# Joint attention of a four-layer gated network, rewritten for products of two rounded parts, two query halves beside each other and steps of two key tiles

## The reference, cut to what matters

```python
H = 16; head_dim = 16
q = x @ Wq + bq
k = concatenate([x @ Wks + bks, context @ Wkc + bkc], axis=1)    # 1024 + 154 keys
v = concatenate([x @ Wvs + bvs, context @ Wvc + bvc], axis=1)
attn = softmax(einsum('bhqd,bhkd->bhqk', q, k) / sqrt(16))
out = einsum('bhqk,bhkd->bqhd', attn, v)
x = x + tanh(gate) * (out @ Wo + bo)
```

## Time and profile before

| | |
|---|---|
| Median of 3 runs (lowest to highest) | 3018.72 us (3017.26 to 3019.69) |
| Profiled execution, time | 3019.72 us |
| Profiled execution, span | 3017.8 us |
| Busy PE / DVE / ACT / POOL | 80% / 66% / 42% / 31% |
| Mean granted TensorE clock | 0.878 of 2.4 GHz |

### The profile page before, as it was taken

One profiled execution on the slowest core, in us unless ns is written; L12 is line 12 of the kernel. 1 busy time (PEld: TensorE's weight loads), 2 busy tenths in 40 slices (PEclk: granted clock), 3 DMA queues, 4 the chain that ended last, 5 costly groups with the idle time before them and its releaser, 6 DMA issues. The chain is left out here.

```text
span 3017.8 us, 43014 instructions
## 1 busy us (share of the span) xinstructions
PE 2415.8 (80%) x15716; PEld 1650.5 (55%) x15716; DVE 1999.3 (66%) x4265; ACT 1255.4 (42%) x2974; POOL 937.4 (31%) x867
## 2 busy tenths in 40 slices
PE   6799999987997899759999776888888987950254
PEld 3233333336886566548888444777666776840122
DVE  4588888824766555457776346775657675579898
ACT  4266666642443544323333112646325564320121
POOL 2000000001554433225554002554335453413343
PEclk9799999996998999869999677899898998975566
DMA  1111111101001000110000001000100000010000
GB/s 71 23 27 27 30 27 27 30 19 47 1 1 58 1 1 1 41 68 1 1 1 4 22 1 47 1 1 12 68 1 1 2 1 32 1 42 0 0 1 28
DMA packets 15681, 57.90 MB, mean 19 GB/s; under 512 B 7408, under 2 KB 7408, under 8 KB 13552
## 3 DMA queue, kind: packets, MB, share of 16 engines
q1 hardware_dynamic: 15472, 55.15, 5.5%
HBM read 39.37 MB, written 2.10 MB: 14 GB/s over the span
## 5 line engine op out<-in xcount | busy, mean ns | idle before, releaser
L2298 ACT ACTIVATE probs<-psum 128x512 f32<-128x512 f32 (+1 forms) x640 | 346.7, 593 | 195.9 <-PE psum L2242 195.0
L2313 DVE TENSOR_REDUCE max_parts<-psum 128x1 f32<-128x512 f32 x512 | 328.6, 684 | 63.4 <-PE psum L2215 59.6
L152 PE MATMUL psum<-x_upper,weights_upper 128*128 128x512 f32 (+2 forms) x624 | 252.8, 405 | 26.6 <-POOL weights_rest L164 17.6
L152 PE MATMUL psum<-x_rest,weights_upper 128*128 128x512 f32 (+2 forms) x624 | 249.8, 400 | 0.0
L152 PE MATMUL psum<-x_upper,weights_rest 128*128 128x512 f32 (+2 forms) x624 | 247.1, 396 | 0.0
L152 PE MATMUL psum<-weights_upper,hidden_upper 128*128 128x256 f32 (+2 forms) x768 | 242.4, 316 | 1.8 <-DVE x_tok L311 1.7
L164 POOL TENSOR_TENSOR weights_rest<-L1f,weights_upper 128x256 fp32r<-128x256 f32 x216 | 181.4, 866 | 183.6 <-ACT weights_upper L269 183.6
L152 PE MATMUL psum<-weights_upper,hidden_rest 128*128 128x256 f32 (+2 forms) x768 | 217.2, 283 | 0.0
L152 PE MATMUL psum<-weights_rest,hidden_upper 128*128 128x256 f32 (+2 forms) x768 | 217.1, 283 | 0.0
L2253 PE MATMUL psum<-probs,v_tok 128*17 128x256 f32 (+1 forms) x2560 | 201.1, 385 | 0.4 <-ACT probs L2298 0.4
L2242 PE MATMUL psum<-q_stack,k_stack 98*128 98x512 bf16 (+1 forms) x640 | 198.3, 387 | 0.5
(11 more groups left out here) (432 smaller groups left out, 6065.4 us busy)
## 6 DMA issues: line engine op xcount, KB each, us to landing
L1f<-in_L1f SPq DMA_DIRECT2D x1, 7936.0 KB, 21.6
k_stack<-k_parts SPq DMA_DIRECT2D x192, 36.8 KB, 2.0
q_stack<-q_parts SPq DMA_DIRECT2D x192, 32.0 KB, 2.0
L0f<-in_L0f SPq DMA_DIRECT2D x1, 4760.0 KB, 14.4
L2f<-in_L2f SPq DMA_DIRECT2D x2, 2268.0 KB, 8.5
L1x<-in_L1x SPq DMA_DIRECT2D x1, 4226.0 KB, 13.2
L2a<-in_L2a SPq DMA_DIRECT2D x2, 2048.0 KB, 11.4
L3f<-in_L3f SPq DMA_DIRECT2D x1, 3072.0 KB, 10.2
```

The source lines that it names most:

```text
L152: ins = pe.matmul(out, lhsT(a).bitcast(F32R), rhs(b).bitcast(F32R), start=start and n == 0, stop=stop and n == len(PASSES) - 1, skip_group ...
L2298: act.activation(pb[0:m, s % NPB, hf * 512:(hf + 1) * 512], net.ps[0:m, STB + hf, :], ACT.Exp, scale=HD ** -0.5).then_inc(exp_done, 1)
L2313: v.tensor_reduce(mx3[:, u % 2, q, k:k + 1], net.ps[:, XB + (2 * n + k) % 3, :], AX.X, ALU.max).then_inc(x_taken, 1)
```

## The change

- Parts. q and k are split into two parts in fp32r. The stack has three combinations of 16 rows (48), and the two rows of maxima make 50.
- Halves. Queries 0 to 511 stand on partitions 0 to 49 of the stack, queries 512 to 1023 on 64 to 113, with the keys copied to both. So each product is two of 512 columns, one for each half, into banks of their own. Stacking a unit still takes 12 transfers: 6 of queries (16 rows x 2 KB) and 6 of keys (16 rows x 4.7 KB, before 2.4 KB). The maxima take four transfers, one per part and half.
- Steps. The five steps of a unit hold two key tiles each: a pair of maxima, two tiles of scores, a pair of maxima, turns, then the value products of the step before's two tiles. Maxima, turned maxima and turned results share a ring of three banks. Four pairs of unit u+2 stand in steps 3 and 4 of unit u, in front of the turn and the split of unit u+1's maxima.
- Exponentials take 1024 columns from two banks. ScalarE also copies the result of a unit out and, once turned, into `o_raw`; dividing by the sum is left to the end of a batch (GpSimd for the first, VectorE for the second).
- Projections and output are three products of rounded parts; biases are added while the results are taken, the output's bias by GpSimd under the heads. The projections go batch by batch, x is transposed there, and the stacks of units 0 to 2 are sent meanwhile.
- The output weights and the context by token become packs of their own (`L0o`, `L3c`); `L3c` is loaded before the last layer.

```diff
--- before.py
+++ after.py
@@ -2049,323 +2058,517 @@
     KT = [P] * (S // P) + CT
     NK = len(KT)
     HC = P // HD
-    Q_PARTS, K_PARTS = [0, 0, 0, 1, 1, 2], [0, 1, 2, 0, 1, 0]
+    Q_PARTS, K_PARTS = [0, 0, 1], [0, 1, 0]
     ROWS = HD * len(Q_PARTS)
+    HALF = 64
...
-        qp = net.sb(attn, "q_parts", [P, 3, C, B, S], BF16)
-        kp = net.sb(attn, "k_parts", [P, 3, C, B, KEYS], BF16)
+        vt = net.sb(attn, "v_tok", [P, B, NK, H, HD + 1])
+        qs = net.sb(attn, "q_stack", [P, NST, S // 2])
+        ks = net.sb(attn, "k_stack", [P, NST, KEYS])
+        qp = two(attn, "q_parts", [P, C, B, S])
+        kp = two(attn, "k_parts", [P, C, B, KEYS])
...
+        def stack(sp, u):
+            b, h = head(u)
+            c, r0 = h // HC, (h % HC) * HD
+            s = u % NST
+            for r, (i, j) in enumerate(zip(Q_PARTS, K_PARTS)):
+                for e in range(2):
+                    lo = HALF * e + r * HD
+                    sp.dma_start(qs[lo:lo + HD, s, :], qp[i][r0:r0 + HD, c, b, e * 512:(e + 1) * 512])\
+                        .then_inc(stacked[s], 16)
+                    sp.dma_start(ks[lo:lo + HD, s, :], kp[j][r0:r0 + HD, c, b, :]).then_inc(stacked[s], 16)
...
+            w = Weights(net, ctx, "L0x")
+            w_out.load()
...
+            layer_norm(net, x, None, keep=xn)
...
+            @block.sync
+            def _(sp):
+                sp.wait_ge(ones_in, 3)
+                sp.wait_ge(taken, 5)
+                for u in range(NST):
+                    stack(sp, u)
...
-                        ins = pe.matmul(net.ps[:, n % 4, 0:m], wt[:, k, c * P:(c + 1) * P], src(k),
-                                        start=k == 0, stop=k == C - 1)
+                        ins = three(pe, net.ps[:, IB + n % 4, 0:m], [p[:, k, c * P:(c + 1) * P] for p in wp[name]],
+                                    [p[:, k, :] for p in src], k == 0, k == C - 1)
                     ins.then_inc(made, 1)
...
+                for b in range(B):
+                    turn_x(b)
+                    for n in range(PER):
+                        project(b * PER + n)
+                    for k in range(NK):
+                        values(b, k)
...
+                    for n in range(b * PER, (b + 1) * PER):
+                        _, bias, c, _, out, m = items[n]
+                        v.wait_ge(part_upper, n + 1)
+                        v.scalar_tensor_tensor(out[1].bitcast(F32R), net.ps[:, IB + n % 4, 0:m], w(bias)[:, c:c + 1],
+                                               out[0], ALU.add, ALU.subtract).then_inc(taken, 1)
+                    v.wait_ge(ones_in, 1)
+                    for k in range(NK):
+                        m = KT[k]
+                        v.wait_ge(v_made, b * NK + k + 1)
+                        heads = lambda ap: ap.rearrange("p (h d) -> p h d", d=HD)
+                        v.tensor_tensor(vt[0:m, b, k, :, 0:HD], heads(net.ps[0:m, VB + k % 4, 0:D]),
+                                        heads(w("bvs" if k < S // P else "bvc")[0:m]), ALU.add).then_inc(v_taken, 1)
...
+            NPB, STEPS, AHEAD = 4, NK // 2, 4
+            ST, RING, NR, PVB = 0, 4, 3, 7
...
+            pairs = [("self", j, k) for j in range(4) for k in range(2)] + [("ctx", i, 0) for i in range(2)]
+            NPAIR = len(pairs)
+            ring = [("max", 0, i, e) for i in range(NPAIR) for e in range(2)] + [("top", 0)]
+            ring += [("max", 1, i, e) for i in range(AHEAD) for e in range(2)]
+            at_step = {}
+            for u in range(NU):
+                for k in range(STEPS):
+                    n = u * NPAIR + NPAIR + AHEAD + 2 * k
+                    here = [divmod(m, NPAIR) for m in (n, n + 1) if m < NU * NPAIR]
+                    at_step[u, k] = here
+                    for v_, i in here:
+                        ring += [("max", v_, i, e) for e in range(2)]
+                    if k == 2 and u > 0:
+                        ring.append(("out", u - 1))
+                    if k == 3 and u + 1 < NU:
+                        ring.append(("top", u + 1))
+            ring.append(("out", NU - 1))
...
                 for u in range(NU):
...
+                    n = place["top", u]
+                    sp.wait_ge(reduced, n + 1 - outs_before[n])
...
+                        for e in range(2):
+                            row = HALF * e + ROWS + r
+                            sp.dma_start(qs[row:row + 1, s, :], part[4 * e:4 * e + 4, u % 2, :]).then_inc(rows_in[s], 16)
+                    if u >= 1 and u + 2 < NU:
+                        sp.wait_ge(st_done, 2 * NK * u)
+                        stack(sp, u + 2)
...
+                def enter(item):
+                    n = place[item] - NR
+                    if n >= 0:
+                        if ring[n][0] == "out":
+                            pe.wait_ge(out_taken, outs_before[n] + 1)
+                        else:
+                            pe.wait_ge(reduced, n + 1 - outs_before[n])
+                def max_pair(u, i):
                     s = u % NST
+                    kind, a, k = pairs[i]
+                    if i == 0:
                         pe.wait_ge(stacked[s], 12 * 16 * (u // NST + 1))
...
+                    for e in range(2):
+                        enter(("max", u, i, e))
+                    if kind == "self":
+                        for e in range(2):
+                            r = slice(HALF * e, HALF * e + ROWS)
+                            pe.matmul(bank(("max", u, i, e)), qs[r, s, a * P:(a + 1) * P].bitcast(F32R),
+                                      ks[r, s, k * 512:(k + 1) * 512].bitcast(F32R), start=True, stop=True)\
+                                .then_inc(made, 1)
...
                 def turn_max(u):
+                    enter(("top", u))
+                    pe.wait_ge(max_done, u + 1)
+                    pe.transpose(bank(("top", u))[0:QT, 0:P], mx[:, u % 2, :], net.ident[:]).then_inc(made, 1)
...
                 def scores(u, k):
...
+                        pe.wait_ge(rows_in[s], 64 * (u // NST + 1))
+                    if n >= 2:
+                        pe.wait_ge(exp_done, n - 1)
+                    for e in range(2):
+                        r = slice(HALF * e, HALF * e + ROWS + 2)
+                        pe.matmul(net.ps[0:m, ST + 2 * (k % 2) + e, :], ks[r, s, k * P:k * P + m].bitcast(F32R),
+                                  qs[r, s, :].bitcast(F32R), start=True, stop=True).then_inc(st_done, 1)
...
+                    pe.wait_ge(exp_done, n + 1)
+                    if k == 0 and u > 0:
+                        pe.wait_ge(o_copied, u)
...
+                for u in range(NU):
+                    for k in range(STEPS):
+                        here = at_step[u, k]
+                        for v_, i in here[:1]:
+                            max_pair(v_, i)
+                        scores(u, 2 * k)
+                        scores(u, 2 * k + 1)
+                        for v_, i in here[1:]:
+                            max_pair(v_, i)
+                        if k == 2 and u > 0:
+                            turn_out(u - 1)
+                        if k == 3 and u + 1 < NU:
+                            turn_max(u + 1)
+                        n = u * STEPS + k - 1
+                        if n >= 0:
+                            for m in range(2):
+                                weighted(n // STEPS, 2 * (n % STEPS) + m)
...
+                        n, m = u * NK + k, KT[k]
+                        if n >= NPB:
+                            act.wait_ge(pv_done, n - NPB + 1)
+                        act.wait_ge(st_done, 2 * (n + 1))
+                        act.activation(pb[0:m, n % NPB, :], net.ps[0:m, ST + 2 * (k % 2):ST + 2 * (k % 2) + 2, :]
+                                       .rearrange("p a n -> p (a n)"), ACT.Exp, scale=HD ** -0.5).then_inc(exp_done, 1)
+                        if k == 1 and u > 0:
+                            copy_out(u - 1)
+                        if k == 5 and u > 0:
+                            take_out(u - 1)
...
+                    for e in range(2):
+                        v.wait_ge(made, place["max", u, i, e] + 1)
...
+                def split_max(u):
+                    if u >= 2:
+                        v.wait_ge(rows_in[(u - 2) % NST], 64 * ((u - 2) // NST + 1))
+                    v.wait_ge(made, place["top", u] + 1)
+                    src = bank(("top", u))[0:QT, 0:P]
+                    v.tensor_scalar(hi[:, u % 2, :].bitcast(F32R), src, -1.0, None, ALU.mult).then_inc(hi_done, 1)
+                    v.wait_ge(hi_done, u + 1)
+                    v.scalar_tensor_tensor(lo[:, u % 2, :].bitcast(F32R), src, -1.0, hi[:, u % 2, :], ALU.mult,
+                                           ALU.subtract).then_inc(reduced, 1)
...
+                for u in range(NU):
+                    for k in range(STEPS):
+                        for v_, i in at_step[u, k]:
+                            reduce_pair(v_, i)
```

(56 more changed lines are left out.)

536 lines of the change are left out of this document (270 added, 266 removed).

## The result

The changed kernel takes 2999.36 us (median of 14 runs, 2987.94 to 3014.72), the kernel before 3018.41 in runs on the same chips: ratio 0.9941, 95% interval 0.9925 to 0.9956. So it is faster by 0.6%, where 2.3% was forecast, and its time lies above the range. Its runs spread over 27 us; the fastest had a mean granted clock of 0.865, the slowest of 0.851. The profiled execution took 2995.63 us.

A forecast was written before the change was run, and what follows sets the result against it. TensorE's column stream bounded the old kernel; SyncE's queue would bound the new heads. Start -33.3, heads -27.0, output -12.5, later stages +1.3 gave -71.5 from 3019.72: 2948 us, range 2895 to 2992.

The forecast's parts named there:

- the chain through SyncE: Heads: sending maxima 2.9, stacking issues 6.9, landing 2.1, then 3.44 to the next send make 15.5 us a unit.
- The projections: Start of the kernel: shorter TensorE work, ending at 73.2 us, first maximum at 75.2, stacks of units 0 to 2 hidden underneath.
- The output: Output projection after the heads: 20.3 us, where it took 32.8 before, a gain of 12.5.
- units 1 to 29 at 15.5: Heads: each of these units takes 15.5 us between sends of maxima, 449.5 in all; before, 16.11 a unit.
- rival A: The main forecast, SyncE's queue closing the loop in the heads: 2948 us, own range 2933 to 2963; 50%.
- T(0): Moment SyncE starts to send unit 0's maxima: forecast 88.3 us, was 121.58, with 13.1 from first maximum as before.
- T(0) to T(1): Start of the heads, from sending unit 0's maxima to sending unit 1's: 13.8 us, as stacks are already there.
- rival E: Heads: TensorE's clock falls to its lower level for good, a unit takes some 20 us, total 3078; 10%.
- Without SyncE's chain 13.8: Heads: if SyncE's queue did not close the loop, a unit would take 10.35 + 3.44 = 13.8 us.
- Rival B: Heads: the queue does not close the loop, the unit falls to 13.8 us, total 2899; 14%.
- Rival C: Heads: half-height products don't overlap for 50 rows of 512 columns, unit about 16.3 us, total 2971; 12%.
- Rival D: Heads: stacks land later because key rows are larger, up to 1.5 us a unit, total 2991; 14%.

The follow-up runs named there:

- turn_single: Changed kernel with the next unit's maxima turned before the wait for stacks, and each half of a maxima pair waiting only for its own bank: 2916.56 us, ratio 0.966.
- half_stacks: Changed kernel, from unit 3 on sending only the six stacking transfers of the first row half: 2951.59 us, ratio 0.9778.
- start_busy: Changed kernel with unread filler products at the start of the heads, five before the first maximum and four after each of unit 0's pairs: 2998.59 us, ratio 0.9939.
- turn_first: Changed kernel with step 3 turning and splitting the next unit's maxima before the first pair of maxima of unit u+2: 2943.69 us, ratio 0.9758.
- turn_fill: turn_first with two unread products between the bank waits of each self maxima pair and five at the start: 3024.92 us, ratio 1.0027.
- split_pool: Changed kernel with the six stacking transfers of the second row half sent from GpSimd's queue instead of SyncE's: 3022.69 us, ratio 1.0012.
- turn_spread: turn_single with value products of one key tile between the halves of each step's second maxima pair: 3026.93 us once, 3222.5 three times.

## Why the prediction was wrong

The direction of the whole and the chain through SyncE were right; the time was 51 us too low, and in the heads the direction was wrong. That the kernel is faster all the same comes from the start and the output, not from the heads. Step by step:

- **The projections** were right: first maximum at 75.06, forecast 75.2, the stacks ready under them. **The output** took 22.8, forecast 20.3; two low stretches of 3.4 us lie in it. Before it took 33.7 (640.71 to 674.4), where the sum has 32.8. **Later stages** took 2.4, forecast 1.3.
- **The step that failed: units 1 to 29 at 15.5.** The chain itself (rival A) is confirmed: 15.62 to 15.64 in undisturbed units, 0.63 a transfer up and down, and gone when the pair is moved behind the turn. But the average was 16.63: 29 x 1.13 = 33 of the 51 us (against the profiled runs, 47 us; T(0), T(0) to T(1), the output and the later stages make up the rest). The chain's own 0.12 a unit is 3.5 us of them. Two terms were put at nothing. The first is the clock, rival E, in a milder form than forecast: stretches of 3.4 to 20.5 us at 0.50 and not the whole of the heads. They cost about 14 us: 11.2 in seven units, in which TensorE came late to the pair that needs the stacks, and 2.4 between that pair and the next send. The idling in the waits lets the clock fall: filled, it was 1.00; lengthened, it was lower. I had set little on E by the cross attention, where TensorE idles a tenth of the time; but a share says nothing of single waits, which here last 0.3 to 1.8 us. The second are the long issues (10.7 us) and late landings (4.5 us), which the eleven equal steps of the earlier trace rows didn't show.
- The Trainium skill (TensorE: Matmul & The Clock Gate, HAM oscillation) says that a wait for a transfer repeated in every tile can throttle the clock each time. The trace agrees in kind: 11 of 12 stretches come with such a wait. It differs in size: the waits of the page's case are given as about 3 to 5 us, those here were 0.65 to 1.8, so that the prediction's "each unit" went further than the page; the level returned within 3.4 to 20.5 us, and in several units it didn't fall.
- **T(0) = 88.3** was 92.1. "The same after" was wrong: two halves that enter the ring of three together leave 0.3 of idling in each of ten pairs. T(0) to T(1) took 21.1, forecast 13.8; the low level held until 110, and turn_single shows the sum of both, 89.5 and 14.55.
- **"Without SyncE's chain 13.8"** was 14.9 (half_stacks). It is not TensorE's work, which is 10.9 by the low unit of start_busy, forecast 10. Of the 1.1 the order of the turn and the pair is 0.5 (turn_first 14.47) and the pairs that stop VectorE another 0.5 (turn_single 14.0). Rival B's 2899 was out of reach; the chain cost 0.7 a unit at full clock, not 1.7.
- **Rival C** is refuted: four products of 512 columns in half-height pairs take 0.58 until the next pair begins (348.21 to 348.79), which would be 0.92 without overlap. The Trainium skill (TensorEngine Tiling (Array Packing), Key Properties) says that changing the tiling mode drains the array; the 0.66 for two full-height products in turn_fill agrees, 0.2 for the two changes around them.
- **Rival D** is a fraction: key rows land after 2.4 to 2.5 us, forecast 2.1, and in a few units after up to 3.7. That the transfers also crowd each other only showed in split_pool.

Open is why waits of like length let the clock fall in some units and not in others, what let it fall in turn_first without a wait for a transfer, what ended the low level in turn_spread at 373.5 us, and whether the instruction transfers really are what makes issues long; no run here was made for that.

## What to carry to other kernels

When a change makes TensorE's work shorter, draw the new loop through the queues first, and then ask where the saved time goes: here it went into two short waits a unit, and these cost a second time through the clock. A single line of order (what stands ahead of the turn) was worth three times the whole change. Take apart waits that ask for two buffers at once when the ring is only one longer, and don't mend the clock with filler that can outlast the wait.

## What the runs showed of the hardware that was not expected

- TensorE can stay at 0.50 while busy 100% of the time for 297 us (turn_spread; 27 us in start_busy). Three further runs of turn_spread took 3222.5 against 3026.9 us; that they stayed low for longer is likely but not shown.
- Transfers from two queues crowd each other: landing went from 2.4 to 2.8 and 3.4 us, some issues from 0.6 to 1.1 and more, and the rows of maxima came 0.5 us later, and with them the unit at full clock.
- Some issues of SyncE take 1.1 to 1.7 us instead of 0.6; a 16 KB transfer of the instruction queue began beside each of the 13 in the heads of the changed kernel.
- In the changed kernel all eight waits for the stacks of 1.39 us or more were followed by a stretch at 0.50, and three of ten shorter ones.
